# Up products of the seventh shared chunk placed ahead of the expert tiles, held in the row buffers

## The chip, the cores and the metric

The kernel runs on one core of a Trainium2 chip. The time is that of one execution on the device, in microseconds (us), as the median of the runs shown. The engines are TensorE (PE in the profile; PEld is its weight load), VectorE (DVE), ScalarE (ACT), GpSimd (POOL) and SyncE (SP). SP and ACT also issue plain DMAs, GpSimd issues the indirect ones.

## What is computed

The reference, cut to what matters: image patches become tokens, one attention layer follows, and then a mixture of experts with a shared expert beside it.

```
h = tokens(x) joined with txt                    # 16 x 193 rows of 128
h = h + attention(layernorm(h))
xt = layernorm(h)
shared = silu(xt @ sw1) * (xt @ sw3) @ sw2       # every row
scores = xt @ gate_w.T                           # 8 experts, the best 2 chosen
p = sigmoid(top 2 scores); p = p / sum(p)
y[e] = (silu(xt @ w1[e]) * (xt @ w3[e])) @ w2[e] # for the rows that chose e
out = h + sum over the two choices of p * y + shared
```

## The kernel before

The rows of `h` are kept in `hrow`, 25 tiles of up to 128 rows: three to each of eight groups `g` (a pair of images), and one, `CLS`, with the 16 class rows. Every engine has its program written out by hand, and semaphores alone tie them together; nothing is scheduled by a planner, so the order of the calls in the code is the order on the engine.

**Routing.** Behind the attention the normalised rows are gated, each row's place in its two experts' lists is counted, and GpSimd scatters the rows to `xs_dram` (line 778, 50 indirect DMAs). VectorE works out a table of the expert tiles: first the columns `tab_cols`, which TensorE turns (line 1536), then `tab` (line 1149, it counts `tab_done` to 1). Behind that it works out `tab_n` (lines 1154 to 1158, `tab_done` to 2) and `by_slot`, the two best scores in order (lines 1159 to 1167, `raw_best` and five more, `top_done`), from which ScalarE takes an exponential (line 691) between two table loads. SP waits for `tab_done` and for all scatters, and then loads the rows of the first eight tiles (line 391).

**Expert tiles.** 56 tiles of 128 rows run in a pipeline over all engines (`expert_steps`). In step t TensorE does `up` of tile t-2 (line 1565), `transposed` of tile t (line 1556), `hidden` of tile t-3 (line 1574) and `down` of tile t-4 (line 1585). VectorE splits the transposed rows in two (lines 1190 and 1192) and multiplies the two halves (line 1203), ScalarE does the silu and two copies, GpSimd scatters the results to `y_dram` (line 789).

**Shared expert.** It is done in nine chunks `c`: eight of 384 rows and one of 16. For each chunk and each half `m` of the hidden width, `shared_up(c, m)` on TensorE makes two products (lines 1473 and 1476) in the two banks that `up_banks(c, m)` names, `shared_silu` on ScalarE takes the silu of one into `sh_s[m]`, and `shared_mul` on VectorE multiplies by the other into `sh_h[m]` (line 1055). `shared_down(c)` takes both halves to bank 3 (line 1488), and `shared_add(c)` adds the bank to `hrow` (line 1061). Six chunks, 0 to 5, run ahead of the tiles, among the routing; `EARLY` = 6, 7 and 8 run behind them. `shared_up` of a product two back in a row has to have been multiplied, `shared_down(c)` needs `shared_add(c - 1)`, and TensorE waits for `sh_add` 6 ahead of the first tile.

**End.** SP loads the results of the first choices (`y_rows[:, 0]`) and then of the second choices back in five pieces, `CHUNKS`, of six tiles, the last one `CLS` alone (line 417). VectorE adds the weighted first choices to `hrow` (`first_results`, line 1221) and, with ScalarE's help (`second_results`, line 730), the second ones (`all_results`, lines 1234 and 1239). Each `all_results(c)` releases the stores of piece c: pieces 0 and 1, four DMAs each, from SP; of pieces 2 and 3 two DMAs each from SP (line 424) and two each from ACT (line 747); piece 4, one DMA, from SP.

Of the kernel before, what the change touches and what calls it, by code (L numbers as in the profile page):

```python
# [10 lines left out]
ALU = mybir.AluOpType  # L11
# [3 lines left out]
P = 128  # L15
# [5 lines left out]
D = 128  # L21
# [4 lines left out]
G = B // 2  # L26
# [6 lines left out]
J = 3 * G + 1  # L33
# [63 lines left out]
def build(nc, patches, txt, w_tok, cls, pos, wqk, bqk, small, gate_b,  # L97
# [4 lines left out]
    with ctx:  # L102
# [122 lines left out]
        CHUNKS = [(a, min(a + YC, J)) for a in range(0, J, YC)]  # L225

# [72 lines left out]
        def up_banks(c, m):  # L299

            return [(5, 7), (2, 1), (4, 0)][(2 * c + m + (1 if c >= EARLY else 0)) % 3]

        SH = G + 1

# [4 lines left out]
        EARLY = 6  # L309
# [32 lines left out]
        def _(sp):  # L342
# [87 lines left out]
        def _(act):  # L430
# [257 lines left out]
            shared_silu(5, 1)  # L688

# [44 lines left out]
            shared_silu(EARLY, 0)  # L734
            shared_silu(EARLY, 1)
            shared_silu(EARLY + 1, 0)
            second_results(0)
            shared_silu(EARLY + 1, 1)
            second_results(1)
            shared_silu(EARLY + 2, 0)  # L740
            shared_silu(EARLY + 2, 1)
            for c in range(2, len(CHUNKS) - 1):
                second_results(c)
            for c in range(2, len(CHUNKS)):
                act.wait_ge(fin_done, c + 1)
# [49 lines left out]
        def _(dve):  # L795
# [253 lines left out]
            def shared_mul(c, m):  # L1049
# [3 lines left out]
                if m == 0:  # L1053
                    after(dve, sh_down, c)
                V.tensor_tensor(sh_h[m][:, 0:n], sh_s[m][:, 0:n], bank[up_banks(c, m)[1]][:, 0:n], ALU.mult  # L1055
# [78 lines left out]
            shared_add(3)  # L1134
            shared_mul(4, 1)
# [16 lines left out]
            shared_add(5)  # L1152
            for k in range(2):
# [5 lines left out]
            raw_best(G - 1)  # L1159
            then(V.tensor_tensor(swap[:], ix8[:, :, 0], ix8[:, :, 1], ALU.is_gt))  # L1160
            dve.wait_ge(raw_done, J)
            then(V.tensor_scalar(keep[:], swap[:], -1.0, 1.0, ALU.mult, ALU.add))
            best = raw8[:, :, 0:2].rearrange("p j k -> p k j")
            V.tensor_tensor(part[:, 0], best, keep[:].rearrange("p (k j) -> p k j", k=1).broadcast_to([P, 2, J]), ALU.mult)
            then(V.tensor_tensor(part[:, 1], best[:, ::-1, :], swap[:].rearrange("p (k j) -> p k j", k=1)
                                 .broadcast_to([P, 2, J]), ALU.mult))
# [482 lines left out]
```

## Time and profile before

| | us |
|---|---|
| median of 3 runs | 264.31 |
| lowest and highest | 263.71 and 264.48 |
| the profiled execution, own time | 264.31 |
| its span in the profile | 262.5 |
| TensorE busy | 233.8 (89%) |
| VectorE busy | 189.9 (72%) |
| ScalarE busy | 155.3 (59%) |
| GpSimd busy | 115.2 (44%) |

The span begins with the first instruction and ends with the last; 1.8 us of the execution lie around it. The profile's timeline has the attention up to about 127 us, the shared chunks 0 to 5 among the routing up to 155.5, the tiles from 157.0 to 243.7 and the end of the kernel from there to 262.5. Times below are from the span's start. The granted clock of TensorE is given as a share of its full 2.4 GHz; 0.50 is 1.2 GHz.

### The profile page before, as it was taken

The numbers are of one execution on the slowest core, as the hardware profiler recorded it, in microseconds if no ns is written. First come the engines' busy times: TensorE is split into PE (matmuls) and PEld (weight loads), VectorE is DVE, ScalarE is ACT, GpSimd is POOL, SyncE is SP. The second block draws the span as 40 slices with busy tenths as digits, with TensorE's granted clock in tenths as the row PEclk, the third lists the DMA queues.
The fourth block names the chain that finished last, engine by engine and source line by source line (L and its number), as shares of the span: only waits on it lengthen the run. The fifth ranks groups of instructions, "written<-read, shape, count | busy, mean of one in ns | idle before, by whom it ended". The sixth has DMA issues, their size and how long they took to land.

```text
span 262.5 us, 5589 instructions
## 1 busy us (share of the span) xinstructions
PE 233.8 (89%) x1491; PEld 192.2 (73%) x1491; DVE 189.9 (72%) x737; ACT 155.3 (59%) x436; POOL 115.2 (44%) x121
## 2 busy tenths in 40 slices
PE   0499799999999999989899957999999999999960
PEld 0477688888879797966566636888888888888640
DVE  1533998798989898987988767766666666665784
ACT  0325458585858585875974325666666666666571
POOL 1400000055646464640656720676666666676600
PEclk9999799999999999997999997999999999999996
DMA  6989964143434301010011412324323332348736
GB/s 199 318 271 338 333 241 149 39 122 126 117 127 121 136 21 44 20 40 2 31 42 50 135 43 52 93 62 113 85 82 91 85 98 75 99 112 236 202 99 181
DMA packets 31421, 31.68 MB, mean 121 GB/s; under 512 B 4322, under 2 KB 27403, under 8 KB 30496
## 3 DMA queue, kind: packets, MB, share of 16 engines
q1 hardware_dynamic: 25960, 23.95, 30.7%
q0 software_dynamic: 3392, 6.36, 7.4%
q10 hardware_dynamic: 2040, 1.04, 1.4%
q8 instruction: 13, 0.21, 0.4%
q14 instruction: 16, 0.13, 0.2%
HBM read 22.80 MB, written 9.03 MB: 121 GB/s over the span
## 4 chain that ended last, share of the span: by engine, by line
PE 80%; DVE 9%; ACT 5%; ACTq 3%; issue 2%; DVEq 0%
PE bank L1565 15%; PE bank L1281 12%; PE bank L1585 10%; PE bank L1296 5%; PE bank L1574 5%; PE bank L1488 3%; PE bank L1473 3%; PE bank L1476 3%; PE bank L1369 2%; PE bank L1556 2%; PE bank L1329 2%; PE bank L1373 2%; PE bank L1295 2%; PE bank L1327 2%; PE bank L1355 2%
## 5 line engine op out<-in xcount | busy, mean ns | idle before, releaser
L778 POOL DMA_INDIRECT xs_dram<-xd,pos_i x50 | 54.9, 1099 | 82.7 <-DVE pos_i L967 69.9
L789 POOL DMA_INDIRECT y_dram<-att,goal x56 | 56.4, 1007 | 37.7 <-ACT att L713 37.4
L1281 PE MATMUL bank<-wt,xp_both 128*128 128x128 f32 x288 | 38.6, 288 | 0.0
L1281 PEld LDWEIGHTS bank<-wt,xp_both 128*128 128x128 f32 x288 | 36.9, 201 | 1.4 <-issue 0.7
L699 ACT ACTIVATE att<-bank 128x256 f32<-128x256 f32 x56 | 21.5, 383 | 24.9 <-PE bank L1565 24.9
L1585 PE MATMUL bank<-w_sb,att 128*128 x224 | 34.5, 277 | 0.0
L1190 DVE CAST xsT_h<-bank 128x128 fp32r<-128x128 f32 x56 | 16.3, 292 | 24.9 <-PE bank L1556 24.9
L1585 PEld LDWEIGHTS bank<-w_sb,att 128*128 128x128 f32 x224 | 29.4, 191 | 0.3 <-issue 0.2
L1565 PE MATMUL bank<-xp_both,xsT_h 128*128 x56 | 27.3, 488 | 1.5 <-DVE xsT_l L1192 1.5
L1203 DVE TENSOR_TENSOR att<-att,bank 128x256 f32<-128x256 f32 x56 | 23.0, 411 | 1.6 <-ACT att L699 1.6
L1565 PE MATMUL bank<-xp_both,xsT_l 128*128 x56 | 22.6, 403 | 0.0
L1565 PE MATMUL bank<-w,xsT_h 128*128 x56 | 22.4, 401 | 0.0
L1574 PE MATMUL bank<-cst,att 128*128 128x128 f32 x112 | 21.7, 276 | 0.3 <-DVE att L1203 0.3
L706 ACT COPY att<-bank 128x256 f32<-128x256 f32 x56 | 20.8, 372 | 0.7 <-PE bank L1574 0.7
L1574 PEld LDWEIGHTS bank<-cst,att 128*128 128x128 f32 x112 | 14.1, 142 | 5.3 <-DVE att L1203 0.8
L1192 DVE TENSOR_TENSOR xsT_l<-bank,xsT_h 128x128 fp32r<-128x128 f32 x56 | 16.3, 292 | 1.9
L713 ACT COPY att<-bank 128x128 f32<-128x128 f32 x56 | 14.9, 266 | 4.6 <-PE bank L1585 0.6
L1296 PE MATMUL bank<-wqk_sb,xT 128*128 128x256 f32 x48 | 16.9, 434 | 0.0
L1488 PEld LDWEIGHTS bank<-sw_sb,sh_h 128*128 128x128 f32 (+1 forms) x100 | 11.7, 188 | 6.9 <-issue 4.5
L1556 PE MATMUL bank<-cst,xs_all 128*128 128x128 f32 x56 | 15.4, 277 | 1.5 <-DMA xs_all<-xs_dram 1.5
L1488 PE MATMUL bank<-sw_sb,sh_h 128*128 128x128 f32 (+1 forms) x100 | 13.2, 280 | 3.5 <-DVE sh_h L1055 2.2
L625 ACT ACTIVATE sh_s<-bank 128x384 f32<-128x384 f32 (+1 forms) x18 | 8.1, 456 | 13.6 <-PE bank L1476 13.3
(201 smaller groups left out, 497.2 us busy)
## 6 DMA issues: line engine op xcount, KB each, us to landing
xp_both<-in_patches SPq DMA_DIRECT2D x7, 1152.0 KB, 5.2
xs_all<-xs_dram SPq DMA_DIRECT2D x56, 64.5 KB, 1.8
xd<-y_dram SPq DMA_DIRECT2D x8, 384.0 KB, 4.6
w<-in_w SPq DMA_DIRECT2D x2, 1024.0 KB, 9.7
y_dram<-att,goal POOLq DMA_INDIRECT x56, 2.3
xs_dram<-xd,pos_i POOLq DMA_INDIRECT x50
hrow<-in_txt SPq DMA_DIRECT2D x2, 384.0 KB, 10.4
out_tokens<-hrow SPq DMA_DIRECT2D x6, 128.0 KB, 1.9
```

Of the source, the lines that this page charges most:

```text
L699: A(hs[q][:], bank[2 + q][:, 0:HID], ACT.Silu).then_inc(silu_done[at], 1)
L706: nc.scalar.copy(hmT[q][:], bank[4 + q][:, 0:HID].rearrange("p (m t) -> p m t", m=2)).then_inc(hmT_done[at], 1)
L778: nc.gpsimd.indirect_dma_start(out=xs_dram[:, :], out_offset=bass.IndirectOffsetOnAxis(ap=pos_i[0:rows, j, k:k + 1], axis=0), in_=xd[0:row ...
L789: nc.gpsimd.indirect_dma_start(out=y_dram[:, :], out_offset=bass.IndirectOffsetOnAxis(ap=goal[u][:, 0:1].bitcast(I32), axis=0), in_=ys[u][ ...
L1203: V.tensor_tensor(hm[q][:], hs[q][:], bank[2 + q][:, HID:2 * HID], ALU.mult).then_inc(hm_done[at], 1)
L1281: M(ps[:, 0:D], xp[p][:, k, :], wt[:, k, :], start=(k == 0), stop=False)
L1296: return M(ps, lhs, wqk_sb[:], start=False, stop=True)
L1488: last = M(bank[3][0:rows, D * t:D * t + D], sh_h[m][:, P * t:P * t + rows], sw2_sb[:, m, :], start=(m == 0), stop=(m == 1))
L1556: T(bank[q][:, 0:P], xs[u][:, 0:D], ident).then_inc(tx_done[slot(u, 0)], 1)
L1565: last = M(bank[2 + q][:, 0:2 * HID], x[q][:], w[:, bass.ds(first * 2, 2 * HID)], start=(i == 0), stop=(i == 2))
L1574: last = T(bank[4 + q][:, P * m:P * m + P], hm[q][:, P * m:P * m + P], ident)
L1585: last = M(bank[6 + q][:, 0:D], hmT[q][:, m, :], w[:, bass.ds(first + m * D, D)], start=(m == 0), stop=(m == 1))
```

## The change

Chunk 6 is split. Its up products, silus and multiplications now stand ahead of the tiles, behind those of chunk 5; as `sh_h` is in use there, the two halves go to `xrow[0]` and `xrow[1]`, the row buffers of the attention, which are free by then (`hidden_of`). Its down product and its add stay behind the tiles, where they now come first. The wait of TensorE for `sh_add` 6 moves from ahead of the first tile to ahead of `up` of the second; ahead of the first stands a wait for the new multiplications. The block of VectorE that makes `by_slot` moves up, behind `shared_add(3)`, and `shared_add(5)` moves down, behind `tab_n`. On ScalarE the silus of chunk 6 come ahead of the exponential. Behind the tiles the order of VectorE is new, and the class rows' piece 4 is finished and stored ahead of piece 3 (`FINISHED`).

```diff
+        FINISHED = (0, 1, 2, 4, 3)
...
-            return [(5, 7), (2, 1), (4, 0)][(2 * c + m + (1 if c >= EARLY else 0)) % 3]
+            return [(5, 7), (2, 1), (4, 0)][(2 * c + m + (2 if c > EARLY else 0)) % 3]
...
+        def hidden_of(c, m):
+            return xrow[m][:].rearrange("p t d -> p (t d)") if c == EARLY else sh_h[m]
...
-            for c in range(len(CHUNKS)):
-                sp.wait_ge(fin_done, c + 1)
+            for turn, c in enumerate(FINISHED):
+                sp.wait_ge(fin_done, turn + 1)
...
             shared_silu(5, 1)
+            shared_silu(EARLY, 0)
+            shared_silu(EARLY, 1)
...
             act.wait_ge(weight_done, 1)
-            shared_silu(EARLY, 0)
-            shared_silu(EARLY, 1)
             shared_silu(EARLY + 1, 0)
+            shared_silu(EARLY + 1, 1)
             second_results(0)
-            shared_silu(EARLY + 1, 1)
-            second_results(1)
             shared_silu(EARLY + 2, 0)
             shared_silu(EARLY + 2, 1)
+            second_results(1)
...
             shared_add(3)
+            raw_best(G - 1)
...
+            V.tensor_tensor(by_slot[:], part[:, 0], part[:, 1], ALU.add).then_inc(top_done, 1)
             shared_mul(4, 1)
...
             remainder_w13(7)
-            shared_add(5)
+            shared_mul(EARLY, 0)
+            shared_mul(EARLY, 1)
...
-            raw_best(G - 1)
...
+            shared_add(5)
...
             first_results(1)
-            shared_mul(EARLY, 0)
-            shared_mul(EARLY, 1)
+            shared_add(EARLY)
+            shared_mul(EARLY + 1, 0)
             first_results(2)
-            shared_mul(EARLY + 1, 0)
-            shared_add(EARLY)
             shared_mul(EARLY + 1, 1)
-            all_results(0)
             dve.wait_ge(sh_add, EARLY + 1)
             first_results(3)
+            all_results(0)
...
             first_results(4)
-            for c in range(2, len(CHUNKS)):
-                all_results(c)
+            all_results(2)
+            all_results(4)
+            all_results(3)
...
             shared_up(5, 1)
+            shared_up(EARLY, 0)
+            shared_up(EARLY, 1)
             shared_down(EARLY - 1)
-            pe.wait_ge(sh_add, EARLY)
+            pe.wait_ge(sh_mul, 2 * EARLY + 2)
             pe.wait_ge(tab_done, 1)
...
                 pe.wait_ge(xsT_done[at], turns(n, u, 2))
+                if U * n + u - 2 == 1:
+                    pe.wait_ge(sh_add, EARLY)
...
-            shared_up(EARLY, 0)
+            shared_up(EARLY + 1, 0)
             for k in range(SLOTS):
                 pe.wait_ge(ys_done[k], TILES // SLOTS)
-            for c in range(EARLY, SH):
-                shared_up(c, 1)
-                if c + 1 < SH:
-                    shared_up(c + 1, 0)
-                shared_down(c)
+            shared_down(EARLY)
+            shared_up(EARLY + 1, 1)
+            shared_up(EARLY + 2, 0)
+            shared_up(EARLY + 2, 1)
+            shared_down(EARLY + 1)
+            shared_down(EARLY + 2)
```

VectorE behind the add of chunk 3, before the change: the multiplication of chunk 4's second half follows at once, and then the columns of the table. In these lists `sh_h` and `sh_s` are the buffers of the shared expert, and line 1061 is its add.

```order
L1055 TENSOR_TENSOR sh_h0<-sh_s0,bank0 128x384
L1061 TENSOR_TENSOR hrow<-bank3,hrow 128x384
L1055 TENSOR_TENSOR sh_h1<-sh_s1,bank7 128x384
L1136 TENSOR_SCALAR t_w<-tf 128x8
L1137 SCALAR_TENSOR_TENSOR te<-cst,tf 128x8
```

The same place of VectorE in the changed kernel, where the lines are four further on:

```order
L1059 TENSOR_TENSOR sh_h0<-sh_s0,bank0 128x384
L1065 TENSOR_TENSOR hrow<-bank3,hrow 128x384
L928 MAX raw8<-sc 128x8 x4
L1140 TENSOR_TENSOR swap<-ix8 128x25
L1142 TENSOR_SCALAR keep<-swap 128x25
L1144 TENSOR_TENSOR part<-raw8,keep 128x50
L1145 TENSOR_TENSOR part<-raw8,swap 128x50
L1147 TENSOR_TENSOR by_slot<-part 128x50
L1059 TENSOR_TENSOR sh_h1<-sh_s1,bank7 128x384
L1149 TENSOR_SCALAR t_w<-tf 128x8
L1150 SCALAR_TENSOR_TENSOR te<-cst,tf 128x8
```

The block of `by_slot` now stands between that add and that multiplication.

VectorE ahead of the first tile, before the change, from the multiplication of chunk 5's second half; the block of `by_slot` goes on for one more row to the first tile's `xsT_h0`:

```order
L1055 TENSOR_TENSOR sh_h1<-sh_s1,bank0 128x384
L1070 TENSOR_TENSOR w13<-w13,xp_both 128x512
L1061 TENSOR_TENSOR hrow<-bank3,hrow 128x384
L1154 TENSOR_SCALAR t_n<-cst,te 128x8 x2
L1156 CAST tab_n<-t_n 128x16
L1157 TENSOR_SCALAR tab_n<-tab_n 128x16
L1158 TENSOR_SCALAR tab_n<-tab_n 128x16
L924 MAX raw8<-sc 128x8 x4
L1160 TENSOR_TENSOR swap<-ix8 128x25
L1162 TENSOR_SCALAR keep<-swap 128x25
L1164 TENSOR_TENSOR part<-raw8,keep 128x50
L1165 TENSOR_TENSOR part<-raw8,swap 128x50
```

The same place of VectorE in the changed kernel, down to the first tile:

```order
L1059 TENSOR_TENSOR sh_h1<-sh_s1,bank0 128x384
L1074 TENSOR_TENSOR w13<-w13,xp_both 128x512
L1059 TENSOR_TENSOR xrow0<-sh_s0,bank7 128x384
L1059 TENSOR_TENSOR xrow1<-sh_s1,bank1 128x384
L1168 TENSOR_SCALAR t_n<-cst,te 128x8 x2
L1170 CAST tab_n<-t_n 128x16
L1171 TENSOR_SCALAR tab_n<-tab_n 128x16
L1172 TENSOR_SCALAR tab_n<-tab_n 128x16
L1065 TENSOR_TENSOR hrow<-bank3,hrow 128x384
L1196 CAST xsT_h0<-bank0 128x128
```

Two multiplications into `xrow` have come in, the block has gone, and the add stands directly ahead of the first tile's cast.

VectorE behind the last tile, before the change (line 1221 is `first_results`, line 1239 the sum of `all_results`):

```order
L1221 SCALAR_TENSOR_TENSOR hrow<-xd,weight,hrow 128x128 x12
L1055 TENSOR_TENSOR sh_h0<-sh_s0,bank1 128x384
L1055 TENSOR_TENSOR sh_h1<-sh_s1,bank0 128x384
L1221 SCALAR_TENSOR_TENSOR hrow<-xd,weight,hrow 128x128 x6
L1055 TENSOR_TENSOR sh_h0<-sh_s0,bank7 128x384
L1061 TENSOR_TENSOR hrow<-bank3,hrow 128x384
L1055 TENSOR_TENSOR sh_h1<-sh_s1,bank1 128x384
L1239 TENSOR_TENSOR hrow<-hrow,xd 128x768
L1221 SCALAR_TENSOR_TENSOR hrow<-xd,weight,hrow 128x128 x6
```

The same place in the changed kernel:

```order
L1227 SCALAR_TENSOR_TENSOR hrow<-xd,weight,hrow 128x128 x12
L1065 TENSOR_TENSOR hrow<-bank3,hrow 128x384
L1059 TENSOR_TENSOR sh_h0<-sh_s0,bank1 128x384
L1227 SCALAR_TENSOR_TENSOR hrow<-xd,weight,hrow 128x128 x6
L1059 TENSOR_TENSOR sh_h1<-sh_s1,bank0 128x384
L1227 SCALAR_TENSOR_TENSOR hrow<-xd,weight,hrow 128x128 x6
L1245 TENSOR_TENSOR hrow<-hrow,xd 128x768
```

Two multiplications are gone, the add of chunk 6 comes first, and the fourth piece of first choices stands ahead of the first sum.

## Rows read from the trace of the kernel before

**Rows 1.** Chain of work that ended last, page, by engine.

```profile
PE 80%; DVE 9%; ACT 5%; ACTq 3%; issue 2%; DVEq 0%
```

**Rows 2.** The page's granted TensorE clock in 40 slices of 6.56 us.

```profile
PEclk9999799999999999997999997999999999999996
```

**Rows 3.** Timeline of TensorE, 149 to 159: start, us, operation [idle before <-releaser].

```profile
149.44 1.58 PE L1488 MATMUL bank<-sw_sb,sh_h 128*128 128x128 f32 x12
...
151.89 0.81 PE L1476 MATMUL bank<-x2T,sw 128*128 128x384 f32 x2
153.95 1.58 PE L1488 MATMUL bank<-sw_sb,sh_h 128*128 128x128 f32 x12 [1.26 <-DVE sh_h L1055]
157.00 0.41 PE L1556 MATMUL bank<-cst,xs_all 128*128 128x128 f32 x2 [1.47 <-DMA xs_all<-xs_dram]
158.95 0.49 PE L1565 MATMUL bank<-xp_both,xsT_h 128*128 x1 [1.55 <-DVE xsT_l L1192]
```

**Rows 4.** Busy us by stretch: PE, PEld, DVE, ACT, POOL, granted clock, DMA share, GB/s.

```profile
160.00:162.00 2.00, 2.00 (x7) 1.50 (x6) 1.07 (x5) 0.56 (x2) 0.00 (x0) 0.50 0.05 12
26.00:29.60 3.60, 2.31 (x19) 1.98 (x17) 3.10 (x7) 1.95 (x6) 0.00 (x0) 1.00 1.09 350
```

**Rows 5.** Timeline of TensorE: one step of the tiles at full clock.

```profile
163.85 0.48 PE L1565 MATMUL bank<-xp_both,xsT_h 128*128 x1
...
164.63 0.27 PE L1556 MATMUL bank<-cst,xs_all 128*128 128x128 f32 x1
164.74 0.38 PE L1574 MATMUL bank<-cst,att 128*128 128x128 f32 x2
...
165.32 0.47 PE L1565 MATMUL bank<-xp_both,xsT_h 128*128 x1
```

**Rows 6.** Waits of SP's queue: waited for, us in total, times, longest.

```profile
SPq L424 <- DVE hrow L1239: 6.6, 3, 5.3
...
SPq L389 <- DMA xs_dram<-xd,pos_i: 1.5, 1, 1.5
```

**Rows 7.** Source view of line 424, SP's stores: ns min/median/max, first and last start.

```profile
L424 SPq DMA_DIRECT2D out_tokens<-hrow x13: 383/586/657, 252.6 to 260.4; - x13
...
DMA to landing us min/median/max: 1.6/1.9/2.4
```

**Rows 8.** Timeline of VectorE, 147 to 158.

```profile
147.03 0.56 DVE L1055 TENSOR_TENSOR sh_h<-sh_s,bank 128x384 f32<-128x384 f32 x1 [0.77 <-PE bank L1488]
147.50 0.55 DVE L1061 TENSOR_TENSOR hrow<-bank,hrow 128x384 f32<-128x384 f32 x1
148.74 0.56 DVE L1055 TENSOR_TENSOR sh_h<-sh_s,bank 128x384 f32<-128x384 f32 x1 [0.69 <-ACT sh_s L625]
...
156.04 0.35 DVE L1154 TENSOR_SCALAR t_n<-cst,te 128x8 f32<-128x8 f32 x2
...
156.93 0.37 DVE L924 MAX8 raw<-sc 128x8 f32<-128x8 f32 x4
...
158.20 0.28 DVE L1190 CAST xsT_h<-bank 128x128 fp32r<-128x128 f32 x1
```

**Rows 9.** Timeline of ScalarE: the silu of chunk 5's second half.

```profile
152.73 0.49 ACT L625 ACTIVATE sh_s<-bank 128x384 f32<-128x384 f32 x1 [2.73 <-PE bank L1476]
```

**Rows 10.** Timeline of TensorE behind the tiles.

```profile
243.73 0.81 PE L1473 MATMUL bank<-x2T,sw 128*128 128x384 f32 x2
...
247.73 1.58 PE L1488 MATMUL bank<-sw_sb,sh_h 128*128 128x128 f32 x12
```

**Rows 11.** Timeline of VectorE behind the tiles.

```profile
247.50 1.66 DVE L1221 SCALAR_TENSOR_TENSOR hrow<-xd,weight,hrow 128x128 f32<-128x128 f32 x6
...
251.63 0.95 DVE L1239 TENSOR_TENSOR hrow<-hrow,xd 128x768 f32<-128x768 f32 x1
...
257.01 0.86 DVE L1234 SCALAR_TENSOR_TENSOR hrow<-xd,weight,hrow 128x128 f32<-128x128 f32 x3
...
258.27 0.33 DVE L1234 SCALAR_TENSOR_TENSOR hrow<-xd,weight,hrow 16x128 f32<-16x128 f32 x1
```

More of the change, by code:

```diff
@@ L299, in up_banks @@
         def up_banks(c, m):
-            return [(5, 7), (2, 1), (4, 0)][(2 * c + m + (1 if c >= EARLY else 0)) % 3]
+            return [(5, 7), (2, 1), (4, 0)][(2 * c + m + (2 if c > EARLY else 0)) % 3]
         SH = G + 1
+        EARLY = 6
+        def hidden_of(c, m):
+            return xrow[m][:].rearrange("p t d -> p (t d)") if c == EARLY else sh_h[m]
         def weighed_by_act(c):
@@ L1052, in shared_mul @@
                 dve.wait_ge(sh_act, 2 * c + m + 1)
-                if m == 0:
-                    after(dve, sh_down, c)
-                V.tensor_tensor(sh_h[m][:, 0:n], sh_s[m][:, 0:n], bank[up_banks(c, m)[1]][:, 0:n], ALU.mult
+                if m == 0 and c != EARLY:
+                    after(dve, sh_down, c - 1 if c == EARLY + 1 else c)
+                V.tensor_tensor(hidden_of(c, m)[:, 0:n], sh_s[m][:, 0:n], bank[up_banks(c, m)[1]][:, 0:n], ALU.mult
                                 ).then_inc(sh_mul, 1)
@@ L1134, in _ @@
             shared_add(3)
+            raw_best(G - 1)
+            then(V.tensor_tensor(swap[:], ix8[:, :, 0], ix8[:, :, 1], ALU.is_gt))
+            dve.wait_ge(raw_done, J)
+            then(V.tensor_scalar(keep[:], swap[:], -1.0, 1.0, ALU.mult, ALU.add))
+            best = raw8[:, :, 0:2].rearrange("p j k -> p k j")
+            V.tensor_tensor(part[:, 0], best, keep[:].rearrange("p (k j) -> p k j", k=1).broadcast_to([P, 2, J]), ALU.mult)
+            then(V.tensor_tensor(part[:, 1], best[:, ::-1, :], swap[:].rearrange("p (k j) -> p k j", k=1)
+                                 .broadcast_to([P, 2, J]), ALU.mult))
+            V.tensor_tensor(by_slot[:], part[:, 0], part[:, 1], ALU.add).then_inc(top_done, 1)
             shared_mul(4, 1)
@@ L1158, in _ @@
             V.tensor_scalar(tab_n[:], tab_n[:], 4, None, ALU.logical_shift_left).then_inc(tab_done, 1)
-            raw_best(G - 1)
[L1160 to L1166, printed above, removed]
-            V.tensor_tensor(by_slot[:], part[:, 0], part[:, 1], ALU.add).then_inc(top_done, 1)
+            shared_add(5)
             def weights(step):
@@ L1262, in _ @@
             first_results(4)
-            for c in range(2, len(CHUNKS)):
-                all_results(c)
+            all_results(2)
+            all_results(4)
+            all_results(3)
         @block.tensor
@@ L1487, in shared_down @@
                     for m in range(2):
-                        last = M(bank[3][0:rows, D * t:D * t + D], sh_h[m][:, P * t:P * t + rows], sw2_sb[:, m, :],
+                        last = M(bank[3][0:rows, D * t:D * t + D], hidden_of(c, m)[:, P * t:P * t + rows], sw2_sb[:, m, :],
                                  start=(m == 0), stop=(m == 1))
```

4 lines of the change are left out of this document (2 added, 2 removed).

## The prediction, made before the changed kernel had run

> **What bounds the kernel now.** I read the chain that ended last first. It is TensorE for 80% [rows 1]: through routing and tiles this engine, and whoever lets it wait, sets the time, and VectorE, ScalarE and the stores set the end.
>
> Next comes the granted clock. It is full nearly everywhere, but three slices read 7 and the last 6 [rows 2]. The third 7, slice 25, covers 157.5 to 164.1, the first tiles. The timeline of TensorE shows what came ahead of it: three waits, 1.26, 1.47 and 1.55 us, with one down product and two transposes between them, so that of the 6.4 us up to 158.95 the engine works some 2 [rows 3]. Then it falls: from 160 to 162 the engine is busy throughout at 0.50, which is 1.2 GHz [rows 4]. It is back at full speed by 163.85, where a step of the tiles takes 165.32 - 163.85 = 1.47 us [rows 5].
>
> The waits of SP show the two ends. The rows of the first tiles wait 1.5 us for the last scatter, so the table is not what is late there. The stores wait three times for VectorE, 5.3 us for the first and 1.3 us for the other two together [rows 6]. Thirteen stores are issued by SP at a median of 0.586 us each, the last at 260.4, and they land 1.6 to 2.4 us later [rows 7]. The last is the small one of the class rows; with the shortest landing it is in at 262.0, and the span ends at 262.5. So the end is SP's issuing once pieces come fast enough: 13 x 0.586 = 7.6 us from 252.6 give 260.2, and 261.0 is when it was through.
>
> **The change, part by part.**
>
> Ahead of the tiles, VectorE. The block of `by_slot` costs 158.20 - 156.93 = 1.27 us. It now follows `shared_add(3)`, whose place holds VectorE until 147.50 + 0.47 = 147.97 (0.47 is the distance of two such instructions, 147.50 - 147.03). VectorE sat idle for 0.69 us there, waiting for ScalarE; the multiplication that started at 148.74 starts at 149.24, 0.50 later [rows 8]. TensorE's down product at 149.44 waits for it, and all behind it moves by 0.50: the table too, and SP has 1.5 us to spare for that [rows 6]. Without that cover each 0.1 us would count fully.
>
> TensorE. The last half of `up(5, 1)` starts at 151.89 + 0.50 = 152.39 [rows 3]. The four new half products take 0.65 each (six halves fill 243.73 to 247.73, with 0.1 left over [rows 10]), 2.6 in all, so the last of them starts at 154.99. ScalarE's silu follows 0.84 behind such a start (152.73 - 151.89), at 155.83, and ends 0.49 later, at 156.32 [rows 9]. The multiplication of 0.47 brings VectorE to 156.79, `tab_n` costs 156.93 - 156.04 = 0.89, to 157.68, and `shared_add(5)` 0.47, to 158.15 [rows 8]. The down product of chunk 5 starts near 155.7 and is through 1.6 later, at 157.3, so the add finds it ready. The first tile's cast stood at 158.20; now 158.15. **The start of the tiles does not move**: 0, within 0.3 either way, since four handovers were summed. The exponential with its table loads has lost its wait for VectorE and is through before the first tile's silu.
>
> So the 2.6 us of products fill waits that were there anyway. TensorE now works through from 149.9 to about 157.5, and one wait of some 1.4 us is left, that for the first tile's two casts. That bears on the **clock**. Before, the fall came behind some 4.3 us of waiting in 6.4; now it would have to come behind one wait of 1.4. I expect it not to come. What it is worth: the steps from the first tile's `up` to the fourth's took 163.85 - 158.95 = 4.90. At full clock they take at most 3 x 1.47 = 4.41, a gain of 0.49. At least: the first has only up products and a transpose, 164.74 - 163.85 = 0.89; the second has the `hidden` product beside them, 0.2 more, 1.1; the third is full, 1.47; 3.46 in sum, a gain of 1.44. In the second step, though, TensorE waits for silu, multiplication and transposed rows of the first tiles, so that it is near a full step. 0.89 + 1.47 + 1.47 = 3.83 gives **1.07**, which I take. From there on the tiles are bound by TensorE, and everything behind them moves by as much.
>
> Behind the tiles. One up product (two halves, 1.3 us) is gone ahead of the down product of chunk 6: it starts at 243.73 + 4.00/3 = 245.1 and is through 1.6 later, at 246.7. `first_results` 0 and 1 are done by then, so VectorE takes the add at 246.7. Then: add 0.47, multiplication 0.47, `first_results(2)` 1.66 less the usual overlap of 0.08, 1.58, multiplication 0.47, `first_results(3)` 1.58: 4.57, so the first sum starts at 251.3 and not at 251.63 [rows 11]. Piece 0 is released 0.3 us earlier, SP starts at 252.3. From there VectorE has the two 16 wide multiplications of the class chunk (an estimate of 0.2 for both), an add of 0.47 and the sum of piece 1, 0.95, to 253.8; SP is busy with piece 0 until 252.3 + 4 x 0.586 = 254.6. It does not wait again: VectorE ends with piece 3, 257.01 to 258.27 before, 1.26 long [rows 11], and reaches its end near 256.7, where 258.6 stood. ScalarE's part has two silus less ahead of it. **VectorE's 1.9 us are not passed on**: SP's queue takes over. Thirteen issues from 252.3: the last starts 12 x 0.586 later, at 259.3, and lands as a big one, 1.9 later, at 261.2, where 262.0 stood. The gain is **0.8**. Its bounds: the landing may take 2.4 (0.3), and with 8.4 us from 252.6 to 261.0, 1.3 of them waits, an issue may cost 0.545 (1.3).
>
> The sum against the profiled execution, whose 264.31 is also the median of the runs: 264.31 - 1.07 - 0.8 + 0 = 262.44; I say 262.5.
>
> **The rivals.** A measurement of this kernel can tell about 0.3%, 0.8 us, from no change.
>
> A: the clock falls all the same, and only the end gains: 264.31 - 0.8 = 263.5. For it: the first 7 of the page came behind a stretch in which TensorE was busy for 2.31 of 3.60 us [rows 4], so a half idle engine is enough. Against: that stretch was full of small products, and here the engine works through. The Trainium skill (TensorE: Matmul & The Clock Gate, Part 1: The HAM clock gate) says that the point at which the gate looks is not tied to the kernel's start and so varies by run; by that rule a run may lose or keep the gain, and no single trace shows it. Its section on HAM oscillation warns of one long gap between products; the trace disagrees, since no gap was over 1.55 us and the clock fell, and by that rule nothing would be won at the tiles.
>
> B: the clock gains, the end doesn't, 264.31 - 1.07 = 263.2: the last stores are bound by the transfers. For it: stores from SP and ACT overlap more than before, since VectorE releases three pieces in 3 us. Against: landings of 1.9 at the median with issues 0.586 apart are not those of a full queue. The Trainium skill (DMA: Bandwidth & Descriptors, Issuing engines are not separate DMA queues) has both on the same DMA engines, with issuing small beside the transfer; by it B would hold.
>
> C, slower: the clock falls earlier. TensorE waits 0.50 more ahead of 149.9; if the fall comes there, four half products and the down product run at half clock: 2.6 and 1.5 us more ahead of the first cast, less what VectorE and ScalarE would wait anyway, about 3 net. Less both gains where the fall is over by the first tile: 264.31 + 3.0 - 1.87 = 265.4. It decides from 2.7 us of delay on. Against: the engine is dense up to 152.5 and before it.
>
> D: neither gain, or the front's handovers cost what one of them gives: 264.3.
>
> **How the numbers follow.** My forecast 0.56, A 0.18, B 0.14, D 0.06, C 0.06. The range 261.6 to 263.9 takes in the forecast with its bounds (a gain of 1.44 and 1.3 gives 261.6, one of 0.49 and 0.3 gives 263.5), B and A with some of its spread, and leaves out D and C. Faster by over 0.3% means under 263.5: the forecast, B and half of A, 0.79. Within 0.3%: the other half of A and D, 0.15. Slower: 0.06.
>
> **What would show it.** In the profile of the changed kernel: the slice at 157.5 reads 9; the first tile's cast stands within 0.3 of 158.2; the fourth tile's `up` starts near 162.8; SP still waits for the last scatter, about 1.0. At the end, counted from TensorE's first up product behind the tiles: first store 8.6 behind it, last sum of VectorE 13.0, last store 15.6, and no wait of SP between stores. Wrong it would be if the clock still reads 0.50 behind the first tile, if the cast is late because the silus of chunk 6 are, or if SP's stores wait or land late.

## The result, and the profile after

| | before | after |
|---|---|---|
| median of 20 runs each, us | 264.56 (263.61 to 266.14) | 262.93 (260.80 to 264.57) |
| ratio after to before | | 0.994, 95% interval 0.9918 to 0.9961 |
| profiled execution, us | 264.31 | 263.96 |
| its span, us | 262.5 | 262.1 |

The changed kernel is faster by 1.63 us, 0.6%; the interval lies below 1 and reaches from 0.4% to 0.8%. Each ratio, here and below, is taken from runs at most 1.5% above the fastest of their kernel, so on the chips with a wide spread it is not the quotient of the medians over all runs. But the two profiled executions differ by 0.35 us only, so the first thing to explain is not the gain but where three quarters of it are hidden in this pair of traces.

The page's granted clock, 40 slices, of the profile after:

```profile
PEclk9999759999999999999999999999999999999995
```

The 7 of slice 25 has gone, and so has the 7 of slice 19, near 120 us; the fifth and the sixth slice (26.2 to 39.3 us) now read 7 and 5, where one 7 stood [rows 2]. The windows of that early stretch, after (busy us of PE, PEld, DVE, ACT, POOL, then the granted clock, DMA share and GB/s):

```profile
28.00:34.00 6.00, 4.45 (x19) 4.02 (x20) 5.76 (x31) 2.93 (x9) 0.00 (x0) 0.68 1.08 337
34.00:38.00 4.00, 4.00 (x12) 2.28 (x12) 1.55 (x5) 0.81 (x2) 0.00 (x0) 0.50 0.36 144
38.00:41.00 3.00, 3.00 (x14) 2.50 (x14) 1.28 (x3) 0.78 (x3) 0.00 (x0) 0.60 0.00 0
...
160.00:162.00 2.00, 1.72 (x8) 1.26 (x8) 1.21 (x7) 0.91 (x2) 0.00 (x0) 1.00 0.46 103
```

and the same early windows of the kernel before:

```profile
28.00:34.00 6.00, 4.51 (x20) 3.70 (x20) 5.83 (x24) 2.51 (x8) 0.00 (x0) 0.72 1.10 328
34.00:38.00 4.00, 4.00 (x25) 3.00 (x23) 3.55 (x16) 2.20 (x5) 0.00 (x0) 1.00 0.76 298
38.00:41.00 3.00, 3.00 (x25) 2.86 (x25) 2.48 (x11) 1.86 (x7) 0.00 (x0) 1.00 0.00 1
```

From 34 to 38 us TensorE is busy throughout in both, with 25 products before and 12 after: at 0.50 each takes twice as long. That is over 100 us ahead of the first edited instruction, and it is the clock alone. Ahead of 143 us the clock was low for 10.2 us after, and before for 3.4 us here and 3.4 us near 120: in sum 3.4 us more after. No edit stands there, and the kernel before can do the same: its trace with unused products added, the second one below, has some 10 us of half clock in the same place and its last `pos_i` at 145.28. The windows at 160 show the other half: 1.00, where 0.50 stood [rows 4].

To compare the traces I cut them at four points that both have: the last of the early `pos_i` reductions on VectorE, the first tile's cast, the `up` products of the first and of the fourth tile, and the first up product behind the tiles.

| stretch, us | before | after | difference | forecast |
|---|---|---|---|---|
| start to last `pos_i` (nothing edited) | 143.28 | 144.67 | +1.39 | 0 |
| to the first tile's cast | 14.92 | 14.87 | -0.05 | -0.05 |
| `up` of tile 1 to `up` of tile 4 | 4.90 | 3.95 | -0.95 | -1.07 |
| to the first up product behind the tiles | 79.88 | 80.08 | +0.20 | 0 |
| from there to the end of the span | 18.77 | 17.79 | -0.98 | -0.8 |

The four edited stretches sum to -1.78, the median of 20 runs gives -1.63, and the first row takes 1.39 of it back in this execution. (The rows leave out the 0.7 us between the cast and the first `up`, which is 0.75 before and 0.74 after.)

The timeline of TensorE after, 149 to 165 us (start, us, operation, and in brackets the idle time before it and what ended it), shows how the products lie in the waits:

```profile
151.31 1.58 PE L1493 MATMUL bank<-sw_sb,sh_h 128*128 128x128 f32 x12 [0.45 <-DVE sh_h L1059]
...
155.69 0.81 PE L1478 MATMUL bank<-x2T,sw 128*128 128x384 f32 x2
156.34 0.81 PE L1481 MATMUL bank<-x2T,sw 128*128 128x384 f32 x2
156.98 1.50 PE L1493 MATMUL bank<-sw_sb,sh_h 128*128 128x128 f32 x12
159.13 0.41 PE L1563 MATMUL bank<-cst,xs_all 128*128 128x128 f32 x2 [0.65 <-issue]
160.28 0.49 PE L1574 MATMUL bank<-xp_both,xsT_h 128*128 x1 [0.75 <-DVE xsT_l L1198]
...
161.10 0.47 PE L1574 MATMUL bank<-xp_both,xsT_h 128*128 x1
...
162.64 0.48 PE L1574 MATMUL bank<-xp_both,xsT_h 128*128 x1
...
164.23 0.48 PE L1574 MATMUL bank<-xp_both,xsT_h 128*128 x1
```

Of the three waits of [rows 3] (1.26, 1.47 and 1.55) two are left, 0.65 and 0.75, and a new one of 0.45 stands ahead of chunk 4's down product, the cost of the moved block; there is no fall behind them. The steps of the first three tiles are 0.82, 1.54 and 1.59 us.

VectorE after, up to the first cast, same columns:

```profile
155.59 0.68 DVE L1074 TENSOR_TENSOR w<-w,xp_both 128x512 fp32r<-128x512 f32 x1
156.41 0.55 DVE L1059 TENSOR_TENSOR xrow<-sh_s,bank 128x384 f32<-128x384 f32 x1
157.70 0.55 DVE L1059 TENSOR_TENSOR xrow<-sh_s,bank 128x384 f32<-128x384 f32 x1 [0.73 <-ACT sh_s L629]
158.17 0.36 DVE L1168 TENSOR_SCALAR t_n<-cst,te 128x8 f32<-128x8 f32 x2
...
159.07 0.55 DVE L1065 TENSOR_TENSOR hrow<-bank,hrow 128x384 f32<-128x384 f32 x1
159.54 0.28 DVE L1196 CAST xsT_h<-bank 128x128 fp32r<-128x128 f32 x1
```

The chain silu, second multiplication, `t_n`, add, cast is the one that the prediction walked: multiplication at 157.70, cast 1.84 behind it (forecast 156.32 to 158.15, 1.83).

SP's waits and its stores after (waited for, us in total, times, longest; then ns min/median/max with first and last start, and the landing):

```profile
SPq L428 <- DVE hrow L1245: 4.4, 1, 4.4
...
SPq L393 <- DMA xs_dram<-xd,pos_i: 1.1, 1, 1.1
```

```profile
L428 SPq DMA_DIRECT2D out_tokens<-hrow x13: 382/554/672, 252.7 to 259.7; - x13
...
DMA to landing us min/median/max: 1.7/2.0/2.4
```

One wait is left where three stood [rows 6]: once the first piece is out, SP never waits again, while VectorE is done with its last sum early:

```profile
251.69 0.94 DVE L1245 TENSOR_TENSOR hrow<-hrow,xd 128x768 f32<-128x768 f32 x1
...
256.55 0.54 DVE L1245 TENSOR_TENSOR hrow<-hrow,xd 128x384 f32<-128x384 f32 x1
```

VectorE ends at 257.1, SP issues until 260.3. Seen from the first up product behind the tiles at 244.31, the first sum starts 7.4 later (7.9 before), the last sum ends 12.8 later (14.9), and the last store is issued 15.4 later (16.7 by [rows 7, 10]).

### The profile page after: what moved, and what is told of

Its sections match the earlier page's. It is cut to its first block, busy times and chain, and to the rows that moved or that the text cites. A ratio compares the mean times of both kernels' runs of the same rounds, so it can differ in the third digit from the quotient of the medians.

```text
span 262.1 us, 5589 instructions
## 1 busy us (share of the span) xinstructions
PE 232.5 (89%) x1491; PEld 191.2 (73%) x1491; DVE 189.7 (72%) x737; ACT 155.3 (59%) x436; POOL 113.3 (43%) x121
## 4 chain that ended last, share of the span: by engine, by line
PE 77%; DVE 12%; ACT 5%; ACTq 2%; issue 2%; DVEq 0%
PE bank L1574 15%; PE bank L1286 12%; PE bank L1594 10%; PE bank L1301 6%; PE bank L1583 5%; PE bank L1493 3%; PE bank L1374 3%; PE bank L1563 2%; PE bank L1478 2%; PE bank L1378 2%; PE bank L1481 2%; PE bank L1300 2%; PE bank L1334 2%; DVE sh_h L1059 2%; PE bank L1332 2%
## 5 line engine op out<-in xcount | busy, mean ns | idle before, releaser
L793 POOL DMA_INDIRECT y_dram<-att,goal x56 | 55.1, 983 | 36.9 <-ACT att L719 36.6
L712 ACT COPY att<-bank 128x256 f32<-128x256 f32 x56 | 20.8, 372 | 0.9 <-PE bank L1583 0.9
L1301 PE MATMUL bank<-wqk_sb,xT 128*128 128x256 f32 x48 | 17.9, 457 | 0.0
L719 ACT COPY att<-bank 128x128 f32<-128x128 f32 x56 | 14.9, 266 | 4.7 <-PE bank L1594 0.6
L1493 PEld LDWEIGHTS bank<-sw_sb,sh_h 128*128 128x128 f32 (+1 forms) x88 | 10.4, 187 | 6.0 <-issue 2.8
L1493 PE MATMUL bank<-sw_sb,sh_h 128*128 128x128 f32 (+1 forms) x88 | 11.5, 279 | 3.3 <-DVE hrow L1065 1.7
## 6 DMA issues: line engine op xcount, KB each, us to landing
hrow<-in_txt SPq DMA_DIRECT2D x2, 384.0 KB, 10.2
```

The costliest lines, as they stand in the source:

```text
L712: nc.scalar.copy(hmT[q][:], bank[4 + q][:, 0:HID].rearrange("p (m t) -> p m t", m=2)).then_inc(hmT_done[at], 1)
L793: nc.gpsimd.indirect_dma_start(out=y_dram[:, :], out_offset=bass.IndirectOffsetOnAxis(ap=goal[u][:, 0:1].bitcast(I32), axis=0), in_=ys[u][ ...
L1301: return M(ps, lhs, wqk_sb[:], start=False, stop=True)
L1493: last = M(bank[3][0:rows, D * t:D * t + D], hidden_of(c, m)[:, P * t:P * t + rows], sw2_sb[:, m, :], start=(m == 0), stop=(m == 1))
```

## The experiments

Two theories had to be told apart for each half of the gain. For the tiles: the clock fell because TensorE stood idle ahead of them, and the work in the waits keeps it up (mine); or the 0.95 us comes from something else that moved, and the clock would fall by chance (rival A). For the end: SP's issuing sets it (mine), or the transfers, or VectorE. The first two groups of four ran on two chips on which every version took some 280 us or more (the kernel before had medians of 283.77 and 284.87 us over all its runs there); every ratio is taken against the kernel before on the same chip, and the traces are compared stretch by stretch. The last group ran on a chip where the kernel before took 264.67 us, like the one of the result. The changed kernel itself was run again on the first chip only. Each stretch is read from one trace per kernel.

### The products alone, in the kernel before

Two products of chunk 6 are put into each of the two waits of the kernel before, into banks whose contents nobody reads. Nothing else is moved: their results are not used, and chunk 6 is still computed behind the tiles.

```diff
             shared_up(5, 1)
+            filler(0)
             shared_down(EARLY - 1)
+            filler(1)
```

> The kernel before with one thing added: the two up products of chunk 6 are computed a second time, unused, into banks 5 and 7 in TensorE's waits ahead of the tiles, one ahead of the down product of chunk 5 and one behind it. Nothing else moves and the end is as before. Theory 1 (the clock): TensorE's clock stays full at the first tiles, from the first tile's up to the fourth's takes about 3.9 and not 4.9, so about 1.0 us less than before, ratio 0.996. Theory 2 (only the shorter end pays, a fall of the clock is not tied to these waits): no change or up to 0.3 us more than before.

Measured: ratio 0.9994 (0.9927 to 1.0061), which says nothing at this width. In the trace the clock stays at 1.00 behind the first tile, the first to the fourth `up` are 3.95 apart (4.90 before), and the end is the old one, 18.78. The same kernel was run again with the last group, on the quieter chip:

> The kernel before with the unused products in the waits ahead of the tiles once more, beside the others. Theory 1: first to fourth tile 3.95, the end 18.8 as before, about 1 us less than before, ratio 0.996. Theory 2 (all the gain is in the end): 1.000.

Measured: 264.29 us, ratio 0.9966 (0.9926 to 1.0006), 0.9 us; in the trace 3.96 between the tiles and 18.83 at the end. Its interval just touches 1, so the time alone does not show the gain, but both traces do, this one and the one on the slower chip. It also tells something on the waits (TensorE, same columns as above):

```profile
157.36 0.81 PE L1482 MATMUL bank<-x2T,sw 128*128 128x384 f32 x2
158.01 0.81 PE L1483 MATMUL bank<-x2T,sw 128*128 128x384 f32 x2
158.99 0.41 PE L1565 MATMUL bank<-cst,xs_all 128*128 128x128 f32 x2 [0.17 <-issue]
160.95 0.50 PE L1574 MATMUL bank<-xp_both,xsT_h 128*128 x1 [1.55 <-DVE xsT_l L1192]
161.28 0.40 PE L1574 MATMUL bank<-w,xsT_h 128*128 x1
```

The wait of 1.55 us directly ahead of the tiles is still there, as long as in [rows 3], and no fall follows. So that wait alone was not enough; with the waits ahead of it filled the clock stayed.

The single runs show the same gain another way. Runs of one kernel differ in their mean granted clock, and sorted by it, after the fact, they fall into groups. On this chip:

| mean clock of the run | before, median us (runs) | with the products, median us (runs) |
|---|---|---|
| 0.985 | none | 262.4 (4) |
| 0.976 to 0.980 | 264.1 (8) | 263.9 (3) |
| 0.971 to 0.974 | 264.8 (6) | 265.6 (5) |
| 0.964 to 0.968 | 266.2 (9) | none |

Each kernel has three levels, and with the products the whole ladder stands one rung higher: best 262.4 against 264.1, worst 265.6 against 266.2. At one and the same clock they cost nothing or a little. The steps between rungs are 0.7 to 1.7 us; that each is one more fall is a reading of the mean clock, since only one run of each kernel has a trace.

### The same order, with little in the products

The changed kernel, but chunk 6's up products are cut to 32 columns (part of the shared expert of chunk 6 is left out). The order, the waits and the edits at the end are all kept.

```diff
+                n = 32 if c == EARLY else n
                 x = x2T[:, at:at + n]
```

> The changed kernel with the moved up products of chunk 6 cut to 32 of 384 columns (ScalarE and VectorE still work on the full width, on what the banks hold; that part of the shared expert is left out). TensorE has its three waits back, the end is that of the changed kernel. Theory 1: the clock falls to 0.50 again, first to fourth tile takes 4.9 and not 3.95; as the silus and multiplications come earlier, the first tile's cast can come up to 0.8 us earlier, so 0.1 to 0.3 us more than the changed kernel, some 1.4 less than before. Theory 2: 0.5 to 0.8 us less than the changed kernel, since nothing is lost to the clock.

Measured: ratio 0.9958 (0.9885 to 1.0031). The end is that of the changed kernel, 17.84. At the tiles the fall is back. TensorE:

```profile
158.50 0.39 PE L1482 MATMUL bank<-x2T,sw 128*128 128x32 f32 x2
161.54 1.85 PE L1494 MATMUL bank<-sw_sb,sh_h 128*128 128x128 f32 x12 [2.65 <-DVE sh_h L1059]
...
165.04 0.79 PE L1575 MATMUL bank<-xp_both,xsT_h 128*128 x1 [0.58 <-DVE xsT_l L1198]
...
166.54 0.78 PE L1575 MATMUL bank<-xp_both,xsT_h 128*128 x1
...
168.46 0.78 PE L1575 MATMUL bank<-xp_both,xsT_h 128*128 x1
...
170.42 0.48 PE L1575 MATMUL bank<-xp_both,xsT_h 128*128 x1
```

The short products leave a wait of 2.65 us, the first product of a tile takes 0.79 and not 0.48 us, and the first to the fourth `up` are 170.42 - 165.04 = 5.38 apart, where the changed kernel has 3.95. So in the trace what keeps the clock is the work in the products, not their place in the order. The expectation was right on the fall and wrong on its size (4.9) and on the cast, which came no earlier (15.82 us behind the last `pos_i`, against 15.86 in the changed kernel on this chip). The run times do not show the 1.4 us: the median is 281.40 us, that of the changed kernel beside it 281.56, and the intervals of both ratios are too wide to tell.

### The old order behind the tiles

The changed kernel with the old order of VectorE and ScalarE behind the tiles and the old turn of the last two pieces. Chunk 6's up products still stand ahead of the tiles.

```diff
-            shared_add(EARLY)
-            shared_mul(EARLY + 1, 0)
             first_results(2)
+            shared_mul(EARLY + 1, 0)
+            shared_add(EARLY)
             shared_mul(EARLY + 1, 1)
+            all_results(0)
             dve.wait_ge(sh_add, EARLY + 1)
             first_results(3)
-            all_results(0)
```

> The changed kernel with the order of VectorE and ScalarE behind the tiles as it was before, as far as it goes without the two multiplications that moved, and the class piece last again. Theory 1: SP's thirteen stores in a row set the end, so the order of VectorE is worth little: within 0.3 us of the changed kernel, the first store even earlier. Theory 3 (the new order of VectorE makes the gain of the end): 0.6 to 1.0 us more than the changed kernel.

(ScalarE's silus and `FINISHED` go back as well; they are left out here. TensorE's order stays that of the changed kernel.) The changed kernel itself ran beside it, to have its ends on the same chip:

> The changed kernel once more, beside the others on the same chip. All theories: about 1.6 us less than before, ratio 0.994, with runs in two groups 1.5 to 2 us apart that go with the mean granted clock of the run (0.968 and 0.976 or more); theory 1 puts the upper group down to a longer stretch at half clock in the first 40 us, where nothing was changed.

Measured: 281.46 us, ratio 0.9948 (0.9883 to 1.0012), with the old order, and 281.56, 0.9974 (0.9929 to 1.0020), with the new. The ends are 17.93 and 17.76 us. So the new order of VectorE and ScalarE is worth 0.17 us, and the other 0.8 of the 0.98 comes with what both kernels share: chunk 6's up products, silus and multiplications gone from the end, and TensorE's new order there. These were not taken apart. With the old order VectorE's first sum starts earlier, 6.83 us behind the first up product and not 7.38, and its last one ends later, 14.24 and not 12.79. Of these 1.45 us the span shows 0.17: SP starts its stores sooner and waits once more between them, and its issuing covers the rest, as forecast. SP's wait for the sums, with the old order and with the new:

```profile
SPq L428 <- DVE hrow L1245: 4.2, 2, 3.3
...
SPq L428 <- DVE hrow L1245: 5.1, 1, 5.1
```

The two groups of runs that were expected 1.5 to 2 us apart, at mean clocks of 0.968 and 0.976 or more, are not to be seen in the twelve runs of the changed kernel here: their clocks lie from 0.961 to 0.980 and do not part into two.

### The table's block back in its old place

```diff
             shared_add(5)
+            raw_best(G - 1)
+            then(V.tensor_tensor(swap[:], ix8[:, :, 0], ix8[:, :, 1], ALU.is_gt))
...
+            V.tensor_tensor(by_slot[:], part[:, 0], part[:, 1], ALU.add).then_inc(top_done, 1)
```

> The changed kernel with the block of by_slot put back to its old place, directly ahead of the first tile. Theory 1: moved up, the block cost only 0.50 of its 1.27 us, since VectorE waited for ScalarE there; put back it costs all of it, so from the last positions to the first tile's cast it takes 15.6 to 15.7 us and not 14.9, and the whole is 0.8 us more than the changed kernel. Rival (the block is hidden in either place): within 0.2 us of the changed kernel.

Measured: ratio 0.9989 (0.9931 to 1.0047). The time says nothing, the trace says two things. VectorE ahead of the first tile:

```profile
165.38 0.55 DVE L1065 TENSOR_TENSOR hrow<-bank,hrow 128x384 f32<-128x384 f32 x1
165.84 0.36 DVE L928 MAX8 raw<-sc 128x8 f32<-128x8 f32 x4
...
166.98 0.21 DVE L1173 TENSOR_TENSOR by_slot<-part 128x50 f32<-128x50 f32 x1
167.10 0.28 DVE L1196 CAST xsT_h<-bank 128x128 fp32r<-128x128 f32 x1
```

The block holds the cast back by 167.10 - 165.84 = 1.26 us, its whole length. And TensorE:

```profile
165.43 0.41 PE L1563 MATMUL bank<-cst,xs_all 128*128 128x128 f32 x2 [1.05 <-DMA xs_all<-xs_dram]
167.85 0.49 PE L1574 MATMUL bank<-xp_both,xsT_h 128*128 x1 [2.01 <-DVE xsT_l L1198]
```

Waits of 1.05 and 2.01 us with two transposes between them: the clock fell in the second tile (0.50 from 169.0 to 172.4; up to up: 0.82, 1.68 and 2.44, 4.94 to the fourth), although all four half products were in place. From the last `pos_i` to the cast it was only 0.2 us longer than in the other kernels on this chip (16.00 to 15.8), less than the forecast of 0.8: VectorE reaches the add ahead of the block, and TensorE the transposes, 14.3 us behind the last `pos_i` and not 15.4, so that 1.07 of the 1.26 us is given back. Of this 1.07, 0.48 is the block gone from further ahead (TensorE's down product of chunk 4 starts 5.89 behind the last `pos_i`, and 6.37 in the next kernel, that with GpSimd's stores). The rest is a wait of VectorE behind that product, 0.25 us here and 1.16 there, which the changed kernel did not have on the chip of the result; so what the block's move is worth there, this run does not tell. That the clock needs the short last wait as well as the products rests on this one trace, the slowest of ten runs; the nine traces of kernels with both halves of the edit, that of the profile after among them, all keep the clock at the tiles.

### Who issues the stores

In the first version GpSimd takes two of the four stores of pieces 0 and 1, so that SP has nine left:

```diff
-                for dst, src in out_views(c)[0::(1 if c < 2 else 2)]:
+                for dst, src in out_views(c)[0::2]:
                     sp.dma_start(dst, src).then_inc(out_sent, 16)
```

> The changed kernel with half of the stores of pieces 0 and 1 (four of SP's thirteen) issued by GpSimd, which is idle by then. Theory 1 (the end is SP's issuing): from TensorE's first up product behind the tiles to the end of the span it takes 16.1 to 16.8 us and not 17.8. Rival (the stores are bound by the DMA engines that all queues share): 17.5 or more.

Measured: 283.33 us, ratio 1.0066 (0.9973 to 1.0159), and an end of 20.8 us. The stores themselves were through early: VectorE's last sum at 12.79, and SP's last store was landed some 16.4 us behind the first up product. The expectation gave 16.1 to 16.8 us to SP's issuing and 17.5 or more to full transfers; and the landings of SP's stores did grow, from a median of 2.0 us to 2.4. But the end is later than the stores, and neither theory has that: SP then waited at the closing barrier, where it had waited for 0.2 us before:

```profile
SPq L102 <- PEq L102: 4.3, 1, 4.3
```

GpSimd had issued its last store 9.3 us ahead of the end of the span (267.85 + 2.81 = 270.7 of 280.0), and neither an engine nor the DMA has work in its last 4 us. That the 4.3 us are GpSimd's closing work behind its own DMAs fits; what it does there the trace doesn't show.

In the second version ScalarE takes three, two of piece 0 and the class piece, and SP has ten:

```diff
-                for dst, src in out_views(c)[0::(1 if c < 2 else 2)]:
+                for dst, src in {0: out_views(0)[0:2], 1: out_views(1), 4: []}.get(c, out_views(c)[0::2]):
...
+            second_results(2)
+            act.wait_ge(fin_done, 1)
+            for dst, src in out_views(0)[2:4]:
+                act.dma_start(dst, src).then_inc(out_sent, 16)
+            second_results(3)
...
-                for dst, src in out_views(c)[1::2]:
+                for dst, src in (out_views(c) if c == 4 else out_views(c)[1::2]):
```

> The changed kernel with three of SP's thirteen stores given to ScalarE's queue: two of piece 0 behind its third piece of second_results, and the class piece ahead of its two stores of piece 3. Theory 1 (SP's issuing sets the end): from TensorE's first up product behind the tiles to the end of the span it takes 16.6 to 17.0 us and not 17.8, about 1 us less than the changed kernel. Rival (the shared DMA engines set it): 17.6 or more.

Measured: 261.27 us over six runs, ratio 0.9888 (0.9845 to 0.9931). The end is 16.55 us, 1.24 less than in the changed kernel (whose end is 17.76 to 17.79 on two chips, and 17.75 in the kernel with two early products on this one), with the same bytes, the same pieces and VectorE's last sum at the same 12.77. The stores of SP in it:

```profile
L428 SPq DMA_DIRECT2D out_tokens<-hrow x10: 373/540/672, 250.9 to 256.6; - x10
...
DMA to landing us min/median/max: 1.9/2.0/2.2
```

The landing is 2.0 us as in the changed kernel, so the transfers did not set that kernel's end, and rival B falls. It was the issuing. The Trainium skill (DMA: Bandwidth & Descriptors, Issuing engines are not separate DMA queues) says that issuing from several engines saves only the sequencer's time, which it calls usually small; here, with 13 stores of 0.55 us in one row against a landing of 2.0, that time was 1.24 us of the span.

### The early falls

Not part of the change, but they hide it in the pair of traces. The two idle stretches of TensorE near 28 and 30 us get products whose results nobody reads, first three in each:

```diff
                 turn_queries(i - 1)
+                if i == 1:
+                    filler()
...
                     gate(i - 2)
+                if i == 1:
+                    filler()
                 turn_rows(i)
```

> The changed kernel with unused products in the two longest waits of TensorE in the first 35 us, three of 384 columns (about 1 us) in each, into a part of bank 6 that is free there. Theory 1 (falls of the clock come behind such waits, and they make the spread between runs): no 0.50 between 28 and 45 us, runs closer together, and a median 0.7 to 1.5 us under the changed kernel. Rival (falls come by the phase of the run, not by the waits): same median and same spread.

Measured: 281.89 us, ratio 1.0022 (0.9978 to 1.0066). In the trace the falls between 28 and 45 us are gone, though one stands at 66 to 70 us, where no other trace has one, and one at 124 to 128. The twelve runs lie within 2.6 us, where the kernel before spread over 11.5 (35 runs) and the kernel with GpSimd's stores over 6.3 (12 runs) on that chip. The ratio shows no gain, while the medians over all runs are 281.89 and 284.87 us; the changed kernel did not run on this chip, so what the products add to it is not shown. Three products took 2.1 us in a wait of 1.4 and so held up what follows. Together with GpSimd's stores:

> Both of the last two in one kernel. Theory 1: the gains add, 2 to 2.5 us under the changed kernel, some 3.5 to 4 under the kernel before, ratio 0.986. Rival: as the changed kernel, 0.994.

Measured: 282.79 us, ratio 1.0075 (1.0008 to 1.0142), an end of 20.72: the loss at the end is that of GpSimd's stores alone, and the gains did not add as expected. Then with two products in each wait, on the quieter chip:

> The changed kernel with unused products in the two early waits of TensorE again, now two of 384 columns in each (1.3 us, which fits; three took 1.95 and came out 0.5 us too long). Theory 1: no 0.50 between 28 and 45 us, a spread of runs well under the kernel's before, and a median 0.5 to 1.2 us under the changed kernel, ratio to before about 0.99. Rival: median and spread of the changed kernel, 0.994.

Measured: 261.86 us, ratio 0.9879 (0.9843 to 0.9915). The same windows as above:

```profile
28.00:34.00 6.00, 5.81 (x29) 3.81 (x29) 5.83 (x22) 2.69 (x8) 0.00 (x0) 1.00 1.08 323
34.00:38.00 4.00, 4.00 (x25) 3.12 (x24) 3.71 (x17) 2.20 (x5) 0.00 (x0) 1.00 0.82 316
38.00:41.00 3.00, 3.00 (x25) 2.74 (x24) 2.33 (x12) 1.65 (x7) 0.00 (x0) 1.00 0.01 4
```

All three at 1.00, and 25 products from 34 to 38 us, as in the kernel before. The start to the last `pos_i` takes 143.49 us, where the changed kernel's trace has 144.67. The runs still fall into two groups, 259.9 to 260.6 at a clock of 0.989 (four) and 261.8 to 263.5 at 0.982 (eight): a fall near 118 to 122 us, which the kernel before has too, comes in some runs and not in others.

Both that helped, together:

> The last two together. Theory 1: gains add, 1.5 to 2.2 us under the changed kernel, ratio to before 0.987.

Measured: **260.64 us (259.40 to 261.15), ratio 0.985 (0.9809 to 0.9891)**. It beats the kernel before by 4.0 us on the same chip, with six runs that all lie below the lowest of that kernel; the changed kernel did not run on it. In its trace the last `pos_i` stands at 142.39 and the end is 16.65 us.

## Why the prediction was right

262.5 was forecast, 262.93 measured, within the range of 261.6 to 263.9, and faster as said. The forecast gain of 1.8 us was taken from 264.31, the measured one of 1.63 from 264.56. That the total came so near is in part luck: the tiles lost 0.20 us that the sum did not have and the clock gave 0.12 less, and the end gave 0.18 more. By its steps:

**The start of the tiles** was forecast at 0, within 0.3; it moved by -0.05. The working held down to its parts: VectorE's multiplications and the add keep their 0.47, and the down product was through before its add. SP's wait for the scatter was forecast at 1.0 and is 1.1. The one wait of 1.4 us that it left ahead of the tiles became two, 0.65 and 0.75. The block's length of 1.27 us is 1.26 where it is put back, but there the cast came only 0.2 us later, so its price in time is not shown.

**The clock** was forecast at 1.07, with bounds of 0.49 and 1.44; the traces have 0.95. The term was 0.12 too large: the first step, taken as 0.89, took 0.82, and the second and third, taken as full steps of 1.47, took 1.54 and 1.59. The mechanism is shown from both sides in the traces, by the products alone in the old kernel (3.95 and 3.96) and by the emptied products in the new one (5.38); the run times confirm only the first of these, and by their groups. Rival A, a fall all the same, came in none of the nine traces of kernels with both halves of the edit (3.94 to 3.96). C, a fall further ahead, was not seen either.

**The tiles** were said to be shifted only. They became 0.20 us longer. It is there in every kernel with a full clock at the tiles on such a chip, in the three built on the changed kernel (80.06 to 80.10; it has 80.08 itself) and in the old one with the products added (80.16), whose tile code is unchanged. So it comes with the clock that stays full, or with what that shifts, and not with the edit's order. Most of it in the changed kernel is a single step, 168.67 to 170.26, of 1.59 us, where the others take 1.47 to 1.49. Ahead of it a weight load waited 0.28 us for its issue; why is open.

**The end** was forecast at 0.8 with bounds of 0.3 and 1.3, and measured 0.98. The mechanism (SP's issuing takes over from VectorE, so the 1.9 us are not passed on) is shown: VectorE's last sum gained 2.09 us and the span 0.98, SP does not wait between stores, and three stores fewer on SP give 1.24 more. The pace was right: (259.7 - 252.7) / 12 = 0.583 against 0.586. The size was off by 0.18, because the first piece came earlier than worked out, 7.4 us behind the first up product and not 7.6: the add of chunk 6, which waits for the down product, started 2.83 us behind it and not 2.97. B is refuted by ScalarE's stores, with landings of the same 2.0 us.

**What the prediction did not see** is the largest single number in the pair of traces, +1.39 us ahead of any edit. It named the early stretch only as an argument for rival A. The early falls lasted 3.4 us in the trace before, 10.2 after and 6.8 in that with ScalarE's stores. The 20 runs of the changed kernel lie in two groups, eleven from 260.8 to 263.13 us at mean clocks of 0.975 to 0.981, with a median of 262.42, and nine from 263.53 to 264.57 at 0.968 and 0.969, with a median of 264.14. That the second group is the one with the long early falls is read from its only trace. The forecast of 262.5 is the first group's time, though it knew of no groups; the profiled execution, 263.96, is of the second. The Trainium skill (TensorE: Matmul & The Clock Gate, Part 1: The HAM clock gate) says that the gate's look is not tied to the kernel's start; two groups of runs of one program, 1.7 us apart, agree with that.

## What to carry to other kernels

Work that must be done anyway is worth more in a wait ahead of a dense stretch than behind it, for two reasons that add up here: it leaves the tail, and it keeps TensorE's clock. Look then at the waits that other engines make in that stretch too: in one trace here a last wait of 2.01 us was followed by the fall although the products were in place. When an engine at the end gets faster, count the issues of the queue behind it: if their sum is longer, move issues to another engine before touching the arithmetic, and measure which: ScalarE's shortened this end by 1.24 us, GpSimd's made it 3.0 longer. And compare traces between points that the edit can't have moved, before believing a span: here one pair of profiles showed 0.35 us of a gain that was 1.6.

## What the hardware showed that was not expected

The clock fell behind waits of which none was over 1.55 us, and did not fall behind one wait of the same 1.55 with dense work ahead of it. With two products per early wait, 1.5 us, whose results nobody reads, the changed kernel was 1.2% ahead of the one before on one chip (0.9843 to 0.9915), and without them 0.6% on another (0.9918 to 0.9961); the two were not run side by side.

DMAs issued by GpSimd near the end were dear: with four stores, 2.8 us of its time, the span ended 20.8 and 20.7 us behind the first up product in two kernels, although the data was there at about 16.4. The cause is open.

On two chips the same kernels took some 19 us longer, 11 or so of them in the tiles (91.5 and not 80 us), at a granted clock of 1.00. In the changed kernel there, TensorE was busy for 65.04 of 70 us of the tiles where it was busy for 69.71 here; the waits of the engines from 165 to 240 us on that chip:

```profile
POOL y_dram L793 <- issue: 8.8, 23, 0.5
...
PE bank L1583 <- DVE att L1209: 4.5, 7, 1.0
ACT att L705 <- issue: 4.2, 10, 0.4
...
DVE xsT_h L1196 <- issue: 3.6, 6, 0.9
```

In the profile after, from 150 to 230 us, the waits of ScalarE's line 705 for issue sum to 0.9 us and VectorE's line 1196 has none. "issue" is time in which an engine waited for nothing that the profile shows; what differs about those chips no run here tells.
